# Reordering the passage between the two blocks of a fused recurrent-attention and mixture-of-experts kernel

## The reference, cut to what matters

```python
xn = _layernorm(x, axis=-1)
s = _L0_attn_ref(xn, ...)            # linear attention, 16 heads
g = _silu(_L0_ffn_ref(xn, ...))      # 8 experts, top 2, and a shared expert
x = x + s * g
xn = _layernorm(x, axis=-1)
s = _L1_attn_ref(xn, ...)            # causal softmax attention with slopes, 16 heads of 16
g = _silu(_L1_ffn_ref(xn, ...))      # 16 experts, top 2, and a shared expert
x = x + s * g
```

## Time and profile before

| | |
|---|---|
| median of 3 runs | 685.59 us (684.63 to 689.01) |
| the profiled execution | 689.09 us, of which the traced span is 686.4 us |
| busy share of the span | PE 89%, PEld 70%, DVE 59%, ACT 47%, POOL 30% |
| mean granted PE clock | 0.972 of full speed |

### The profile page before, as it was taken

One profiled execution on the slowest core, in us unless ns is written; L12 is line 12 of the kernel. 1 busy time (PEld: TensorE's weight loads), 2 busy tenths in 40 slices (PEclk: granted clock), 3 DMA queues, 4 the chain that ended last, 5 costly groups with the idle time before them and its releaser, 6 DMA issues.

```text
span 686.4 us, 12626 instructions
## 1 busy us (share of the span) xinstructions
PE 612.2 (89%) x4114; PEld 480.5 (70%) x4114; DVE 401.8 (59%) x972; ACT 319.6 (47%) x698; POOL 204.0 (30%) x228
## 2 busy tenths in 40 slices
PE   4989998999999999998777979997978769999994
PEld 4868887899988888777455646665656547787663
DVE  6376657555545384757684766563534156666577
ACT  2213334566554334433354434543434458888542
POOL 0237540300005450400220003452456505555400
PEclk9999999999999999999989999999899989999998
DMA  9995563643325320351559526646730304554363
GB/s 320 273 62 171 164 209 96 204 119 116 110 70 181 72 62 1 112 138 30 130 158 211 114 80 174 154 154 181 141 70 3 50 18 142 162 159 140 111 213 106
DMA packets 90167, 88.85 MB, mean 129 GB/s; under 512 B 31407, under 2 KB 82690, under 8 KB 88290
## 3 DMA queue, kind: packets, MB, share of 16 engines
q1 hardware_dynamic: 81706, 69.14, 39.9%
q0 software_dynamic: 7888, 18.79, 8.8%
q10 hardware_dynamic: 512, 0.13, 0.1%
HBM read 51.44 MB, written 36.45 MB: 128 GB/s over the span
## 4 chain that ended last, share of the span: by engine, by line
PE 72%; DVE 15%; DMA 5%; issue 3%; ACT 3%; SPq 1%; POOL 0%; ACTq 0%; DVEq 0%; POOLq 0%
PE bank L925 10%; PE bank L1004 9%; PE bank L1036 6%; PE bank L757 5%; PE bank L1085 4%; PE bank L990 3%; PE bank L1142 3%; PE bank L850 3%; PE bank L945 3%; PE bank L1160 3%; PE bank L1117 3%; PE bank L1017 3%; DMA QS<-mT 2%; PE bank L802 2%; PE bank L1144 2%
## 5 line engine op out<-in xcount | busy, mean ns | idle before, releaser
L646 POOL DMA_INDIRECT slots<-xn,slot_of x64 | 66.1, 1032 | 133.8 <-DVE slot_of L1817 61.8
L2038 DVE TENSOR_REDUCE mneg<-bank 128x2 f32<-128x512 f32 (+1 forms) x96 | 62.6, 685 | 50.4 <-PE bank L1119 49.8
L670 POOL DMA_INDIRECT rets<-results,slot_of x32 | 34.2, 1070 | 108.8 <-DMA results<-ys 69.7
L743 POOL DMA_INDIRECT results_by_token<-ys,logits x47 | 45.5, 967 | 51.2 <-ACT ys L1486 49.9
L1942 DVE TENSOR_TENSOR xgl<-bank,xgh 128x256 f16<-128x256 f32 (+1 forms) x86 | 36.4, 424 | 38.5 <-ACT xgh L1463 37.9
L1568 ACT ACTIVATE exps_first_keys<-bank 128x512 f32<-128x512 f32 x64 | 35.2, 597 | 41.5 <-PE bank L1144 41.3
L1914 DVE TENSOR_TENSOR hf<-bank,sg 128x512 f32<-128x512 f32 x36 | 24.8, 688 | 47.4 <-PE bank L925 47.4
L1142 PE MATMUL bank<-QS,KS 101*128 101x256 bf16 (+1 forms) x256 | 37.7, 263 | 15.0 <-DMA QS<-mT 14.6
L1438 ACT ACTIVATE sg<-bank 128x512 f32<-128x512 f32 x36 | 21.5, 598 | 61.2 <-PE bank L925 61.2
L1117 PE MATMUL bank<-KS,QS 99*128 99x256 bf16 (+1 forms) x256 | 38.4, 259 | 10.4 <-DVE mneg L2038 9.4
L1949 DVE TENSOR_TENSOR hs<-bank,gs 128x176 f32<-128x176 f32 x86 | 29.3, 341 | 26.9 <-ACT gs L1469 23.7
(11 more groups left out here) (236 smaller groups left out, 1633.9 us busy)
## 6 DMA issues: line engine op xcount, KB each, us to landing
xn<-slots SPq DMA_DIRECT2D x86, 128.0 KB, 2.2
projection_parts<-parts SPq DMA_DIRECT2D x8, 768.0 KB, 3.9
QS<-projection_parts SPq DMA_DIRECT2D x16, 384.0 KB
KS<-projection_parts SPq DMA_DIRECT2D x16, 384.0 KB
slots<-zrow SPq DMA_DIRECT2D x1, 6016.0 KB, 27.1
results<-ys SPq DMA_DIRECT2D x39, 128.0 KB, 1.7
x<-in_x SPq DMA_DIRECT2D x8, 512.0 KB, 6.2
rets<-results_by_token SPq DMA_DIRECT2D x8, 512.0 KB, 7.0
```

What stands on the lines that cost most here:

```text
L646: pool.indirect_dma_start(out=slots_dram, out_offset=bass.IndirectOffsetOnAxis(ap=at, axis=0), in_=xn[:, t, :], in_offset=None).then_inc(s ...
L743: pool.indirect_dma_start(out=returned_dram, out_offset=bass.IndirectOffsetOnAxis(ap=returns_to[:, j:j + 1], axis=0), in_=ys1[:, j % YRING ...
L2038: dve.tensor_reduce(mneg[:, qt, first:first + 2 * heads - 1:2], PS[6 + p % 2][:].rearrange("p (n k) -> p n k", n=heads), AX.X, ALU.max, ne ...
```

## The change

It moves calls in the lists of PE, ACT and DVE; no instruction is added or removed, and no operand changes.

- PE: `max_transposes(0)` goes from behind the two first projections to directly behind `values(0)`; `project(6)` goes ahead of `front(1, 2)`.
- ACT: `place_maxima(0)` with its two DMA issues goes from behind `mid_part(4)` to the front of the list behind `values_copy(0)`; `high_part(6)` goes ahead of `mid_part(5)`, and `mid_part(5)` ahead of `x_copies(1, 2)`; `gate(0, 6)` goes ahead of `high_part(7)`.
- DVE: `normalise(1, 2)` goes ahead of `rest_part(4)`; `rest_part(7)` goes behind `combine` 14 and 15.

```diff
@@ tensor engine
             values(0)
-            for j in (4, 5):
-                pe.wait_ge(xt_sb, half(1, 4))
+            max_transposes(0)
+            pe.wait_ge(xt_sb, half(1, 4))
+            for j in (4, 5, 6):
                 project(j, BOUNDARY_BANK[j])
-            max_transposes(0)
             front(1, NCH - 2)
-            for j in (6, 7):
-                project(j, BOUNDARY_BANK[j])
+            project(7, BOUNDARY_BANK[7])
             router(1, NCH - 2)
@@ scalar engine
             values_copy(0)
+            place_maxima(0)
             high_part(4, BOUNDARY_BANK[4])
             high_part(5, BOUNDARY_BANK[5])
             mid_part(4)
-            place_maxima(0)
+            high_part(6, BOUNDARY_BANK[6])
+            mid_part(5)
             x_copies(1, NCH - 2)
-            mid_part(5)
-            high_part(6, BOUNDARY_BANK[6])
+            gate(0, 2 * NCH - 2)
             high_part(7, BOUNDARY_BANK[7])
-            gate(0, 2 * NCH - 2)
             mid_part(6)
             gate(0, 2 * NCH - 1)
             mid_part(7)
@@ vector engine
             read_max(0)
+            normalise(1, NCH - 2, front1)
             rest_part(4, BOUNDARY_BANK[4])
-            normalise(1, NCH - 2, front1)
             rest_part(5, BOUNDARY_BANK[5])
             combine(NTOK - 4)
             combine(NTOK - 3)
             rest_part(6, BOUNDARY_BANK[6])
-            rest_part(7, BOUNDARY_BANK[7])
             combine(NTOK - 2)
             combine(NTOK - 1)
+            rest_part(7, BOUNDARY_BANK[7])
             read_logits(NCH - 2)
             update_x(0, 2 * NCH - 2)
```

## The result

The changed kernel takes 683.5 us (median of 20 runs, 680.03 to 689.03) against 688.22 us for the kernel before (20 runs, 682.35 to 693.77): a ratio of 0.9927, 95% interval 0.9906 to 0.9947, some 5 us less. The prediction's 681.0 us stood on a median of three runs, 685.59 us; as a ratio it was 0.9933. That this meets 0.9927 more closely than the interval can tell is in part luck. The profiled execution of the changed kernel took 680.64 us, with a span of 678.9.

A forecast was written before the change was run, and what follows sets the result against it. The prediction had PE hold 72% of the chain, with DVE the passage's new bound. A gain of 4.15 us up to 355.17 plus 0.5 for the clock made 4.6, from 685.6 to 681.0 us, range 677 to 686.

The forecast's parts named there:

- PE's wait and its low clock go: PE before the rows' transposes: the idle 3.86 us and the low clock behind them go; PE alone gains 5.5 us.
- ACT's free wait, two issues of 1.16 to 1.56 us: ACT: `place_maxima` waits for `read_max` until 332.3 at no cost; its DMA issues then hold ACT to 333.5 or 333.9.
- DVE as the new bound, its steps beside the low parts stretched by 3.1 us: DVE up to sequence 1's first reduction: 6.9 us earlier undisturbed, 3.8 with four steps stretched by POOL's low parts.
- the last one, the update beside low part 7: DVE's `update_x(0, 6)` beside POOL's low part 7, about 344.5: stretched by the mean of 0.36 and 0.86 us.
- the Trainium skill's rule in its full form: DVE and POOL on their shared port pair: four full blocks of 1.2 us, 4.7 us of stretch, gain 2.5 us.
- The clock, 0.5 us: PE from 355.17 on: the low stretch comes earlier, less of it where PE bounds; 0.5 us gained, at most 1.5.
- 0.36: DVE behind the first reduction: `update_x(0, 7)` is free of its 0.36 us stretch, making the gain 4.15 at 355.17.
- The next wait keeps its size: Wait for sequence 1's maxima, 5.73 us: the weights' loads move with the rest; counted as nothing, 1 us either way.
- The rival without collisions: DVE beside POOL's low parts: no steps suffer, 7.8 to 8.8 us gained, about 677.5 us; chance 0.20.
- the 6.9 us that the prediction had worked out without disturbance: DVE's list without stretched steps: the first reduction of sequence 1 starts at 343.0 in place of 349.93.

The follow-up runs named there:

- e4: Changed kernel with the maxima's transposes back behind the two first projections on PE and the two DMA issues behind the first middle part on ACT; ratio to before 0.9932.
- e2: Changed kernel with the normalisation put back behind the first rest part on DVE; ratio to the kernel before 0.9946.
- e8: Changed kernel with the last rest part back ahead of the last two combines on DVE and its high part ahead of the gate on ACT; ratio to before 0.9937.
- e12: Changed kernel in which POOL subtracts only the first 4 of each 256 columns of low parts 4 to 7; ratio to the kernel before 0.9894.
- e5: Changed kernel with the normalisation back behind the first rest part and the third projection back behind the rows' transposes; ratio to the kernel before 0.9936.

## Why the prediction was right, and where not

The range and the sign held, and so did most of the sum.

- *PE's wait and its low clock go.* Right: no wait, 1.04 us of transposes at full clock. The low clock came again behind the two later waits, as forecast (granted 0.50 from 342 to 348), and was gone by 350.
- *ACT's free wait, two issues of 1.16 to 1.56 us.* Right: 1.24 us, and `high_part(4)` began at 332.38 right behind them. The maxima's rows were never waited for.
- *DVE as the new bound, its steps beside the low parts stretched by 3.1 us.* Right in kind and place, all four low parts on the steps that were named: 3.52 us. The term that was too small is the last one, the update beside low part 7, 0.99 us where the prediction took 0.61. The first reduction came 3.95 us earlier by DVE's stretch, 3.8 forecast (at 344.80, just ahead of the 345 to 347 that were named, as the statistics themselves began 1.1 us earlier). By the prediction's estimate the Trainium skill's rule in its full form (SBUF — State Buffer, the two separate sides) would have made 4.7 us of stretch. The trace agrees in kind: the measured 3.52 lies between that and the 3.1 taken from rows. The Trainium skill (SBUF — State Buffer, Who interferes with whom) says that a reduction never contends on this chip. The trace agrees but does not test it: the reduction at 349.84 in the kernel before took 0.68 us beside the low part that ran from 349.73 to 350.94, but it reads a PSUM bank and not SBUF.
- *The clock, 0.5 us.* Too small for the pair of executions shown: from the first reduction to sequence 1's first step on PE the time fell from 28.24 to 26.45 us, 1.79, of which the forecast had 0.5 and 0.36. But this can't be put down to the change, as the last section shows.
- *The next wait keeps its size.* Right: 5.81 against 5.73 us.

Where the account fell short is not in the sum but in what carries it. The prediction put the late rows down to the order of DVE's list, `read_max` and `rest_part(4)` in front of the normalisation. That is one half of it. Counted from the statistics, the normalised rows were done after 8.55 us in the kernel before, 7.05 with everything changed but the maxima (e4), 6.70 with the maxima alone (e9) and 4.73 with both. The other half is that the list stood still: 2.96 us of DVE's pause were the wait for PE's maxima transposes behind two projections, a row that the prediction did not read. Its sum held all the same, because it begins the transposes at 330.63 and `read_max` at 331.4, and so takes this pause away without naming it.

For the first reduction the maxima weigh most: moved alone they shorten DVE's stretch by 3.44 us (e9), and put back alone they lengthen it by 1.77 (e4), so the shares of the edits do not add up. Put back in the changed kernel, the normalisation costs 0.87 us (e2) and the third projection nothing that can be told (e3). The last rest part's move, which had no price of its own in the prediction, costs some 0.9 us (e8). These are shares of DVE's stretch; how the 5 us of the time divide is not shown, as the ratios of e2, e3, e4, e8 and e9 overlap.

The rival without collisions failed because DVE had hardly a pause left, as the prediction argued against it: 2.83 us of pauses gone came with 2.42 us of stretched steps (e9 against the changed kernel). With the low parts cut short DVE's stretch is 7.65 us below the kernel before (e12), which is near the 6.9 us that the prediction had worked out without disturbance.

## What to carry to other kernels

When an engine with a strict list is late, look first for what its list stood still for, and only then at the order of what is queued behind: the wait that one early instruction has on another engine carried most of the gain here (3.44 of 3.95 us on DVE). Closing pauses on DVE also takes away the room in which POOL's work passed unnoticed, so price the overlap of the two before counting the pause as won. The shares of a change's edits are uneven, and one can be negative: undo them one by one.

## What was not expected of the hardware

The same work ran at different clocks from one kernel's profile to another's. From the first reduction of sequence 1 on, all these kernels do the same work on PE, ACT and DVE; yet until PE stood for the maxima of sequence 1 it took 22.56 us in the changed kernel, 22.93 in e8, 24.42 in the kernel before and 25.12 in e4. (The wait behind it, 3.89, 2.36, 3.82 and 3.21 us, varies too, but that is the landing of a DMA and not PE's clock.) Twelve microseconds of that stretch, in e8 and in e4:

```profile
345.00:357.00 12.00, 9.80 (x95) 6.51 (x96) 9.62 (x23) 8.60 (x16) 2.47 (x3) 0.86 0.83 239
```

```profile
345.00:357.00 12.00, 10.63 (x75) 6.55 (x77) 8.91 (x22) 5.47 (x10) 1.26 (x2) 0.55 0.88 239
```

The last column but two is the granted clock, 0.86 against 0.55: in e4 PE did fewer matmuls (75 against 95) in more busy time. Each of these four executions has a piece at 1.2 GHz right behind a pause of PE (1.49 us in e4, 2.05 in the changed kernel, 2.84 in the kernel before, 3.35 in e8); it lasts from about 342 to 355 in e4 and from about 347 to 350 in e8. Where it begins and ends differs, and with it the time, by up to 2.6 us. A single profile of this kernel therefore can't show a gain of that size at its end. A stretch between two events on one engine is less exposed, though not free of it, as the 1.17 us of e5 show.
